# Four graph layers over one dense adjacency: own states share Z with the gathered sums, TensorE counts some row sums, and every row sum is done in the first sweep

## The reference, cut to what matters

```
x += adj @ (h * keep / 0.9)                          # layer 0
deg = clip(rowsum(adj) + 1, 1); n = (adj@h + h)/deg  # layer 1
x += l2norm(relu([h, n] @ W1 + b1))
a = adj + I; d = a.sum(1); s = where(d>0, d**-.5, 0) # layer 2
x += (s[:,None] * a * s[None,:]) @ h @ W2
n = adj @ h / (rowsum(adj) + 1)                      # layer 3
x += [h, n] @ W3.T
```

## Time and profile before

| | us |
|---|---|
| median of 3 runs | 1969.91 (1969.28 to 1970.76) |
| the profiled execution's own time | 1969.59 |
| its span | 1967.8 |
| PE busy | 1911.7 |
| DVE busy | 894.5 |
| DMA, share of the span | mean 341 GB/s |

### The profile page before, as it was taken

How to read it: one execution, slowest core, us unless ns; L and a number is a source line. 1 busy time by engine, 2 the same in 40 slices (tenths; PEclk the granted TensorE clock), 3 DMA queues, 4 the chain that set the end, 5 groups by cost and what they waited for, 6 DMA issues and landing times.

```text
span 1967.8 us, 22013 instructions
## 1 busy us (share of the span) xinstructions
PE 1911.7 (97%) x9096; PEld 690.0 (35%) x9096; DVE 894.5 (45%) x1130; ACT 123.2 (6%) x307; POOL 11.6 (1%) x29
## 2 busy tenths in 40 slices
PE   5899999999999999999999999999999999999998
PEld 1233333333333333333333333333333333333333
DVE  6365777788888855536455466321111110100221
ACT  0000000000000001100000000111000000000100
POOL 0000000000000000000000000000000000000000
PEclk9999999999999999999999999999999999999999
DMA  9999999998888764776766778496999889999898
GB/s 390 420 421 422 420 422 421 421 408 349 335 336 325 306 273 143 290 309 252 308 252 258 282 294 321 182 373 266 381 373 364 344 297 420 364 357 420 350 423 342
DMA packets 93969, 670.63 MB, mean 341 GB/s; under 512 B 11440, under 2 KB 11440, under 8 KB 12976
## 3 DMA queue, kind: packets, MB, share of 16 engines
q1 hardware_dynamic: 92160, 666.94, 83.8%
q0 software_dynamic: 768, 2.10, 0.3%
q10 hardware_dynamic: 944, 0.20, 0.1%
HBM read 667.09 MB, written 2.10 MB: 340 GB/s over the span
## 4 chain that ended last, share of the span: by engine, by line
PE 88%; DMA 9%; DVE 2%; SPq 0%; issue 0%; ACT 0%; POOL 0%; DVEq 0%
PE acc L532 83%; DMA ring<-stream_in 6%; DMA diag<-stream_in 3%; PE Z L573 3%; PE TOP L613 1%; PE HT_DEG L590 1%; PE HT_DEG L604 1%; SPq L311 0%; DVE h L902 0%; SPq L297 0%; ACT y L368 0%; DVE row_sum L940 0%; DVE row_sum L946 0%; DVE squares L864 0%; DVE centred L862 0%
## 5 line engine op out<-in xcount | busy, mean ns | idle before, releaser
L532 PE MATMUL acc<-ring,h 128*64 128x512 f32 x7744 | 1708.0, 595 | 46.2 <-DMA ring<-stream_in 39.6
L532 PEld LDWEIGHTS acc<-ring,h 128*64 128x64 f32 x7744 | 549.1, 137 | 1102.9 <-issue 1032.0
L940 DVE TENSOR_TENSOR row_sum<-row_sum,ring 128x2048 f32<-128x2048 f32 x190 | 435.6, 2292 | 13.7 <-DMA ring<-stream_in 8.4
L894 DVE TENSOR_TENSOR z_sb<-Z,deg_rsqrt 128x256 f32<-128x256 f32 x16 | 6.8, 425 | 330.5 <-PE Z L573 330.4
L532 PE MATMUL acc<-diag,h 128*64 128x512 f32 x448 | 103.2, 593 | 3.6 <-DMA diag<-stream_in 2.1
L940 DVE TENSOR_TENSOR row_sum<-ring 128x2048 f32<-128x2048 f32 x25 | 57.3, 2293 | 71.9 <-DMA ring<-stream_in 70.0
L573 PEld LDWEIGHTS Z<-below,y 128*128 128x128 f32 x512 | 62.0, 191 | 51.2 <-issue 27.6
L375 ACT COPY y<-acc 64x512 f32<-64x512 f32 x45 | 26.2, 582 | 855.8 <-PE acc L532 814.8
L573 PE MATMUL Z<-below,y 128*128 128x64 f32 x512 | 70.5, 281 | 0.9 <-DVE y L1011 0.9
L532 PEld LDWEIGHTS acc<-diag,h 128*64 128x64 f32 x448 | 33.8, 137 | 67.7 <-issue 63.8
L1002 DVE TENSOR_TENSOR x<-TOP,x 128x256 f32<-128x256 f32 x16 | 6.8, 425 | 102.4 <-PE TOP L613 102.4
(11 more groups left out here) (71 smaller groups left out, 412.7 us busy)
## 6 DMA issues: line engine op xcount, KB each, us to landing
ring<-stream_in SPq DMA_DIRECT2D x604, 1024.0 KB, 10.5
diag<-stream_in SPq DMA_DIRECT2D x28, 1024.0 KB, 10.6
x<-x_in SPq DMA_DIRECT2D x4, 512.0 KB, 7.1
h<-u_in SPq DMA_DIRECT2D x4, 512.0 KB, 8.0
x_out<-x POOLq DMA_DIRECT2D x16, 128.0 KB, 5.5
below<-w_in ACTq DMA_DIRECT2D x6, 16.0 KB, 7.4
above<-w_in ACTq DMA_DIRECT2D x4, 16.0 KB, 6.6
bias<-b_in ACTq DMA_DIRECT2D x1, 32.0 KB, 12.1
```

Source lines behind the costliest of these rows:

```text
L532: return nc.tensor.matmul(half_of(bank, half), h[layer % 2][:, J * F:(J + 1) * F], moving, start=start, stop=stop)
L940: nc.vector.tensor_tensor(row_sum[:, :], before, slot(key)[:, :], ALU.add).then_inc(unit_summed, 1 if count > 1 else 2)
```

## The change

Five things change together.

- Row sums: no row is deferred. TensorE counts 21 units of rows 0 to 5 (`PE_SUMS`: six of row 0, five of row 1, down to one of row 5) with `count_unit`, four 64 x 512 matmuls with `picker` as weights, a matrix whose single column of ones puts the sum in line b of the bank `DEG`. The rest is added by DVE in sweep 1. `fold` has one step instead of two, and `count_total` adds the 128 x 1024 total into the same bank. Behind row 15 the bank is copied once, turned by `turn_degrees`, and `degrees` makes all factors in one go.
- Own states: DVE multiplies them by the clipped degree (`scale_own`), `turn_own` transposes that, ACT copies it in two pieces into the upper half of `y`, and `finish` multiplies both halves with the stacked weights. `top`, `take_top` and their bank are gone.
- The partial sums that used to stand in the two halves are added by DVE (`gather_1`, `fold_group` with two steps, `gather_last`) where ACT copied them before (`copy_y`, `copy_group`).
- `turn_own` in sweep 2 stands behind the third unit of a row, not behind the first.
- DVE ends layer 0 of row b-1 and adds its identity after five additions of row b.

```diff
-DEFER = [12, 12, 6, 6, 6, 6, 6, 4, 2] + [0] * 7
 SINGLES = [list(range(LAST, b, -1)) for b in range(ROWS)]
-DEFERRED = [SINGLES[b][:DEFER[b]] for b in range(ROWS)]
+PE_SUMS = [SINGLES[b][1:7 - b] for b in range(6)] + [[]] * (ROWS - 6)
+DVE_SUMS = [[g for g in SINGLES[b] + list(range(b)) if g not in PE_SUMS[b]] for b in range(ROWS)]
...
             def copy_hT(layer, b):
...
-                nc.scalar.copy(hT[n % 2][:, :], HT).then_inc(hT_copied, 1)
+                by_parity = own_y(b, 1).rearrange("p (k l n) -> p l k n", k=2, l=2)
+                for parity in range(2):
+                    turned = HT[parity * F:(parity + 1) * F, :].rearrange("p (k n) -> p k n", k=2)
+                    done = nc.scalar.copy(by_parity[:, parity], turned)
+                done.then_inc(hT_copied, 1)
...
+            def count_unit(key):
+                b = key[1]
+                pick = picker[:, F - 1 - b:2 * F - 1 - b]
+                for k in (0, 2):
+                    for half in range(2):
+                        nc.tensor.matmul(DEG[half * F:(half + 1) * F, :], pick, source_tile(slot(key), k + half),
+                                         start=key == (1, 0, PE_SUMS[0][0]) and k == 0, stop=False)
+            def count_total(b):
+                pick = picker[:, F - 1 - b:2 * F - 1 - b]
+                pe.wait_ge(total_ready, b + 1)
+                for half in range(2):
+                    mm_d = nc.tensor.matmul(DEG[half * F:(half + 1) * F, :], pick,
+                                            row_total[b % 2][:, half * COLS:(half + 1) * COLS],
+                                            start=False, stop=b == LAST)
+                mm_d.then_inc(total_counted, 1)
...
             def turn_own(layer, b):
...
-                pe.wait_ge(*state(layer, b))
+                pe.wait_ge(scaled_ready, n + 1)
...
-            def top(layer, b):
...
+            turn_own(1, 11)
+            pe.wait_ge(weights_loaded, 7 * 16)
             pe.wait_ge(part_copied, PARTS.index((1, 14)) + 1)
-            head_first(2, FIRST_A[0], behind=lambda: (finish(0, LAST), sum_degrees(1, LAST)))
+            head_first(2, FIRST_A[0], behind=lambda: finish(0, LAST))
...
-                for g in range(LAST, b, -1):
-                    if g == b + 1 and DEFER[b]:
-                        sum_degrees(2, b)
+                for i, g in enumerate(sources):
                     await_unit((2, b, g), 1, 2)
                     both((2, b, g), 1, BANK_UP[b], g == LAST, g == LAST, g == b + 1, g == b + 1)
-                    if g == LAST:
-                        if b < LAST - 1 - HEAD:
-                            finish(1, b + 1)
-                        turn_own(1, b)
-                    if g == LAST - 1:
-                        top(1, b)
+                    if i == 0 and b < LAST - 1 - HEAD:
+                        finish(1, b + 1)
+                    if i == 2:
+                        turn_own(1, b)
...
+            def scale_own(layer, b):
+                n = TURNS.index((layer, b))
+                if n >= 2:
+                    dve.wait_ge(hT_done, n - 1)
+                nc.vector.tensor_tensor(by_tile(scaled[n % 2][:, :]), by_tile(own(h[layer % 2], b)),
+                                        spread(of_row(deg_clipped if layer == 1 else degree, b)),
+                                        ALU.mult).then_inc(scaled_ready, 1)
 
             def fold_group(quad, r):
...
-                if opens_row(quad, r):
-                    nc.vector.tensor_tensor(own_y(r, 1), half_of(bank, 1), own_y(r, 1),
-                                            ALU.add).then_inc(group_folded, 1)
-                else:
-                    dve.wait_ge(group_copied, opened((r + 1) // 4, r))
-                    nc.vector.tensor_tensor(own_y(r), acc[bank][:, :], own_y(r), ALU.add).then_inc(group_folded, 1)
+                chain(nc.vector.tensor_tensor(own_y(r, 0), half_of(bank, 0), own_y(r, 0), ALU.add))
+                nc.vector.tensor_tensor(own_y(r, 0), half_of(bank, 1), own_y(r, 0), ALU.add).then_inc(group_folded, 1)
...
-                if b > 0:
-                    end_layer_0(b - 1)
-                    degrees(1, b - 1)
...
                     sum_unit(key, i)
-                    if b == LAST and i in (5, 7, 9, 11):
-                        take_top(1, 14 - (i - 5) // 2)
-                fold(1, b)
-                add_one(b)
+                    if i == 5 and b > 0:
+                        end_layer_0(b - 1)
+                        add_one(b - 1)
+                fold(b)
...
-            end_layer_0(LAST)
-            degrees(1, LAST)
-            take_top(1, LAST)
-            for b in range(LAST, LAST - 1 - HEAD, -1):
+            degrees()
+            scale_own(1, 14)
+            scale_own(1, 13)
+            degree_factors()
+            scale_own(1, 12)
+            scale_own(1, 11)
+            add_one(LAST)
+            end_layer_0(LAST)
+            dve.wait_ge(weights_loaded, 7 * 16)
+            scale_own(1, LAST)
+            gather_1(15)
+            end_layer_1(15, lambda: gather_1(14), lambda: gather_1(13))
+            end_layer_1(14, lambda: gather_1(12), lambda: gather_1(11))
+            for b in (13, 12, 11):
                 end_layer_1(b)
             for b in range(LAST - 1 - HEAD, -1, -1):
                 if b < LAST - 1 - HEAD:
                     end_layer_1(b + 1)
-                take_top(1, b)
-                if DEFER[b]:
...
+                scale_own(1, b)
+                gather_1(b)
             for r in ADDED[:HEAD]:
...
             for b in range(HEAD, ROWS):
-                for r in TOPS_LATE[b]:
-                    take_top(3, r)
                 add_one_again(b)
+                for r in TURNS_LATE[b + 1] if b < LAST else [14]:
+                    scale_own(3, r)
                 end_layer_2(b)
```

More of the change, by code:

```diff
@@ L124 @@
 FREED = {key: n for n, key in enumerate(units_let_go())}
-SUMMED = {key: n for n, key in enumerate(
-    [(1, b, g) for b in range(ROWS) for g in SINGLES[b][DEFER[b]:] + list(range(b))] +
-    [(2, b, g) for b in range(LAST, -1, -1) for g in DEFERRED[b]])}
+SUMMED = {key: n for n, key in enumerate((1, b, g) for b in range(ROWS) for g in DVE_SUMS[b])}
 PROLOGUE = (3, 2, 1, 0)
@@ L159, in gnn_stack @@
         row_sum = sbuf("row_sum", [P, UNIT])
-        row_total = [sbuf(f"row_total{i}", [P, COLS]) for i in range(2)]
+        row_total = [sbuf(f"row_total{i}", [P, 2 * COLS]) for i in range(2)]
         z_sb = sbuf("z_sb", [P, FEATS])
@@ L286, in restored, with gathered @@
             return diag_restored, ADDED.index(b) + 1
-        def opened(quad, r):
-            return sum(opens_row(*group) for group in GROUPS[:GROUPS.index((quad, r)) + 1])
+        def gathered(layer, b):
+            place = ORDER[layer].index(b) + 1
+            return (sums_ready, place) if layer == 1 else (y_copied, place + layer // 2 * ROWS)
         @block.sync
@@ L415, in _ @@
                     norm_root()
-                    if not DEFER[b - 1]:
-                        degree_root()
                 if b == LAST:
+                    act.wait_ge(total_counted, ROWS)
+                    nc.scalar.copy(degree_rows[:, :], DEG[:, :]).then_inc(deg_copied, 1)
+                    degree_root()
                     for r in (14, 13, 12, 11):
@@ L589, in sum_degrees @@
                 for t in range(TPR):
-                    mm_d = nc.tensor.matmul(DEG[:, t:t + 1], row_total[n % 2][:, t * P:(t + 1) * P], ones[:, :],
-                                            start=True, stop=True)
-                mm_d.then_inc(deg_done, 1)
+                    mm_d = nc.tensor.matmul(HT[:, t * ROWS:(t + 1) * ROWS], degree_rows[:, t * P:(t + 1) * P],
+                                            below[:, 0, 0:ROWS], start=True, stop=True)
+                mm_d.then_inc(deg_turned, 1)
@@ L605, in turn_own @@
                 mm_t.then_inc(hT_done, 1)
-            def top(layer, b):
-                n = TOPS.index((layer, b))
-                pe.wait_ge(hT_copied, n + 1)
-                if n >= 1:
-                    pe.wait_ge(top_taken, n)
-                for k in range(2):
-                    mm_t = nc.tensor.matmul(TOP[:, k * 2 * F:(k + 1) * 2 * F], hT[n % 2][:, k * P:(k + 1) * P],
-                                            above[:, layer, :], start=True, stop=True)
-                mm_t.then_inc(top_done, 1)
@@ L1021, in _ @@
             for b in range(ROWS):
-                if b > 0:
-                    end_layer_0(b - 1)
-                    degrees(1, b - 1)
-                units = [(1, b, g) for g in SINGLES[b][DEFER[b]:] + list(range(b))]
+                units = [(1, b, g) for g in DVE_SUMS[b]]
                 count_first = units[0]
```

320 lines of the change are left out of this document (140 added, 180 removed).

## The result

The changed kernel takes 1949.07 us (median of 4 runs, 1948.27 to 1950.49) against 1969.60 us (4 runs on the same chip): ratio 0.9896, 95% interval 0.9881 to 0.9912. The forecast was 1950.7.

The account below looks back on a forecast made before the run. PE, busy 97% of the span, was taken as the bound. Terms 0.3 + 3.3 - 0.2 - 12.6 + 1.5 - 12.3 + 1.1 = -18.9 took 1969.6 to 1950.7 us; range 1945 to 1957, chance 0.70.

Parts of the forecast that it names:

- Prices on PE: PE costs from trace distances: 0.2155 us an instruction, 1.72 a unit, `Z` 0.94, `TOP` 0.64, row sum 0.98, mode change 0.13.
- Start, row 0: Start of sweep 1: thirteenth unit loads just in time, six counts fit into PE's waits; +0.3 us, bounds 0 to +3.
- rival (4): Row 0 of sweep 1: loads break off, sweep 1 begins 3 to 5 us later, 1954 us; included in the forecast's 0.70.
- Does DVE keep up?: DVE additions in sweep 1: DVE stays below PE's 41.6 us a row with 1.2 us margin, so nothing is added.
- Row 15, head of sweep 2: End of sweep 1 into sweep 2: `TOP` and row sum go, `count_total`, `turn_degrees` and a 1.5 us wait come; -0.2 us.
- Rows 10 to 0 of sweep 2: Sweep 2: eleven `TOP` -7.0, nine second row sums -9.6, PE waiting 0.4 us for the turn in ten rows +4.0; -12.6 us.
- Head of sweep 3: Start of sweep 3: `gather_1(0)` delays the identity additions behind it, so the first diagonal unit is late; +1.5 us.
- Rows of sweep 3: Sweep 3: fourteen `TOP` with a mode change each -10.8, row 5's pause gone -1.5; -12.3 us.
- The end: Behind row 15 of sweep 3: two-step fold delays loads +0.4, last fold on the path +0.7; +1.1 us.
- (1): Sweep 2, both heads and behind groups: PE's new waits are longer than forecast; 1960 us (1957 to 1965), chance 0.12.
- (2): Sweep 1 becomes DVE's: rows 1 to 9 each 2 us longer than PE's, gain gone; 1969 us, chance 0.06.
- (3): Counts and totals on PE cost double, 3.45 us a count, if bank halves don't run side by side; 1998 us, chance 0.08.

Follow-up runs that it names:

- the four edits: Changed kernel with 16 counts, sweep 2's turn and each sweep 3 row's first turn right behind `Z`, identities added before `gather_1(0)`: 1937.54 us, ratio 0.9835.

## Why the prediction came out

The mechanism was right in each part but one, the turn of sweep 2, and the sum missed by 2.4 us in the profiled execution and by 1.6 in the median (1950.7 against 1949.07). By its own steps:

- **Prices on PE.** The counts at 0.2155 an instruction held (0.215). So did 1.72 a unit and 0.94 for `Z`. `TOP` in sweep 2 was mis-sized, 0.64 where 0.79 was measured: its start-to-start distance holds one of its two changes of mode. The row sum with its share was 1.07 and measured 1.13. Together 11 x 0.15 + 9 x 0.06 = 2.2 us too little gain, which is the 2.3 by which rows 10 to 0 of sweep 2 came out better.
- **Start, row 0.** Forecast +0.3, measured -0.3 in a profile with the earliest start of eight; the middle of the eight is 60.7, which would be +0.3. So the -21.3 of the table is some 0.7 too good, and the 20.5 between the medians is the better figure. DVE's first addition began at 39.60, and PE worked through row 0 from 41.08 on. The late load of rival (4) did not show.
- **Rows 1 to 5.** 41.53 a row against 41.6 by the sum, +3.2 against +3.3. The run with fewer counts shows the load limit at 40.7 right below, the one with more shows PE's price right above.
- **Does DVE keep up?** It does, with no wait of PE for a total behind the one at the head of row 1. The totals of rows 5 and 6 stand 40.40 us apart (261.10 to 301.50), and DVE is busy for 39.25 of them: 39.2 and 40.4 were forecast. PE's row is 41.52, so the margin is 1.1 where 1.2 was forecast. The run without counts shows what happens when DVE starts with a debt: at 40.40 a row against PE's 41.5 it takes until row 6 to catch up.
- **Row 15, head of sweep 2.** -0.4 against -0.2; the wait for the last turn's copies, forecast as 1.5, is 1.49. The waits for states in the head are 0.79 and 0.88 us where 1.12 and 0.89 stood, so the gathering inside the root waits cost PE nothing.
- **Rows 10 to 0 of sweep 2.** -14.9 against -12.6, by the two prices above. The +0.4 a row for the turn is the step whose size was right and whose cause was wrong: the scaled state was ready at 1166.79 + 0.42 = 1167.21, 8.11 behind the start of `Z` as forecast (8.2), but PE's units ended only at 1160.14 + 6.90 = 1167.04, so the wait is 0.1, and 0.3 of the 0.4 are the price of the turn's place, alone between units with a change of mode on either side. That the sum came out at 0.4 all the same is luck. The prediction had used 0.13 for a change of mode in every other place and did not count it here. The rule of the Trainium skill (TensorEngine Tiling (Array Packing), Key Properties), that a change of tiling mode drains the engine, was cited beside the price and speaks for just this; the two runs with the turn moved agree with it, at 0.15 us a change, though they show the price and not the draining.
- **Head of sweep 3.** +1.9 against +1.5. The order was the cause, as forecast: with the identities ahead of the gathering the wait is gone. Its price was a little low. Read from the timeline's idle time alone, it would have seemed to be half of what it is.
- **Rows of sweep 3.** -12.7 against -12.3: fourteen `TOP` at 0.80 and the pause of row 5, which was listed with 1.55 and cost 1.6 (the row was 31.19 long and is 27.98, with two `TOP` gone from it).
- **The end.** +2.0 against +1.1. The last fold cost the 0.7 forecast (0.85 to 1.57). The rest is between `Z` of row 15 and the last unit: 122.98 us where it was 121.70, +1.3 for the +0.4 forecast. Without the `TOP` products this stretch was 122.08 in the kernel before, with the wait of 1.78 removed 122.20, and with the four edits 121.42; but with the final groups' code unchanged it also lies anywhere between 122.29 and 123.40 (no counts, fewer counts). So the +1.3 is uncertain by about as much as the forecast missed it. What sets the stretch is open; no run changed the order of the loads.

Of the rivals, (1) had waits that are longer: that of the turn is shorter than forecast, those of sweep 3's head and of the folds are longer, by 0.4 and about 1. (2) is excluded by the changed kernel's own rows, 40.40 us on DVE against 41.53 on PE, and (3) by the counts, 1.72 each there and in the run with 36 of them.

## What to carry to other kernels

Put a 128-column job next to another one: alone among 64-column work it pays two changes of mode, 0.3 us beside its own 0.4. When one engine fills another's waits, find the count by rows: here 21 counts are 36 us of work, almost all of it in time that PE would have waited; 15 more cost 25 us in full, 5 fewer give back 3. Price a short instruction or a wait by the distance between two `Z` with and without it: the distance to its neighbour holds only a part of what it disturbs, and a listed idle time of PE can be less than half of a wait (0.82 for 1.9) or nearly all of it (1.78 for 1.93). And before a difference of one microsecond in a stretch is explained, look at the same stretch in runs whose code is the same there: here they differ by 1.1.
